# A routed decoder layer: pad rows written behind each expert's last row instead of ahead of time

## The reference

```
x = layernorm(x + attention(x))                      # low rank scores, one score matrix for all 16 heads
e = minimum(ids // 3125, 3)                          # four experts, chosen by the id
x = layernorm(x + silu(x @ ctx[e].T) * (x @ ctx[e].T) @ ctx[e])
probs = softmax(x @ Wr + br);  e2 = argmax(probs)    # four experts, chosen by a router
x = layernorm(x + max(probs) * ((silu(x @ Wg[e2]) * (x @ Wu[e2])) @ Wd[e2]))   # 256 -> 1024 -> 256
```

## Time and profile before

| | us |
|---|---|
| median of 3 runs | 195.73 |
| the 3 runs | 194.76, 195.73, 196.36 |
| the profiled execution | 194.84 |
| its span, first to last instruction | 192.5 |

### The profile page before, as it was taken

The page is one execution under the profiler, slowest core; times in us unless marked ns, Lnnn a source line. Parts: engine busy times, 40 slices in busy tenths (PEclk is TensorE's granted clock), DMA queues, the critical chain, the costliest instruction groups (busy, mean ns, idle before and its releaser), DMA issues.

```text
span 192.5 us, 3892 instructions
## 1 busy us (share of the span) xinstructions
PE 175.1 (91%) x966; PEld 139.4 (72%) x966; DVE 129.8 (67%) x406; ACT 103.4 (54%) x274; POOL 103.0 (53%) x130
## 2 busy tenths in 40 slices
PE   1999999999999799989999999999999999999810
PEld 0877766367888546668888788888888888888610
DVE  3277878768687878536664454444799977888950
ACT  3138687535477654647664855534555423455530
POOL 7000267744917666528772368850688800376783
PEclk9999999999999999999999999999999999999975
DMA  5999999348997222247554005544050000011010
GB/s 163 354 334 418 376 364 346 102 140 232 353 371 295 93 87 64 74 116 215 171 167 163 0 1 177 171 156 158 0 167 0 0 0 3 0 54 60 22 63 24
DMA packets 15605, 29.14 MB, mean 151 GB/s; under 512 B 1758, under 2 KB 12000, under 8 KB 15458
## 3 DMA queue, kind: packets, MB, share of 16 engines
q1 hardware_dynamic: 13856, 25.68, 40.1%
q0 software_dynamic: 1440, 3.22, 4.7%
q10 hardware_dynamic: 290, 0.01, 0.1%
HBM read 20.41 MB, written 9.28 MB: 154 GB/s over the span
## 4 chain that ended last, share of the span: by engine, by line
PE 71%; POOL 11%; issue 7%; DVE 4%; DMA 3%; ACT 1%; POOLq 1%; DVEq 0%; ACTq 0%
PE bank L502 14%; PE bank L504 13%; PE bank L503 13%; POOL out_tokens L491 5%; PE bank L764 4%; PE bank L589 4%; PE bank L685 3%; PE bank L662 3%; POOL rstd L418 3%; PE bank L620 3%; PE bank L516 2%; PE bank L598 2%; PE bank L734 2%; PE bank L510 2%; DMA x_sorted<-buf,slot 1%
## 5 line engine op out<-in xcount | busy, mean ns | idle before, releaser
L414 POOL TENSOR_TENSOR w_lo<-stage,w_hi 128x512 fp32r<-128x512 f32 x40 | 51.3, 1303 | 34.7 <-ACT w_hi L841 29.9
L962 ACT ACTIVATE gate<-bank 128x256 f32<-128x256 f32 x44 | 16.9, 384 | 48.1 <-PE bank L504 48.0
L1264 DVE TENSOR_TENSOR hid<-bank,gate 128x256 f32<-128x256 f32 x44 | 18.7, 425 | 30.2 <-ACT gate L962 29.9
L502 PE MATMUL bank<-w_hi,xr 128*128 x88 | 35.9, 408 | 1.4 <-DVE xr L1217 1.2
L504 PE MATMUL bank<-w_hi,xr 128*128 x88 | 34.8, 395 | 0.0
L503 PE MATMUL bank<-w_lo,xr 128*128 x88 | 34.7, 395 | 0.0
L502 PE MATMUL bank<-w_hi,hT 128*128 x88 | 28.6, 324 | 0.7 <-DVE hT L1269 0.7
L418 POOL TENSOR_TENSOR rstd<-mv,mhalf 128x1 f32<-128x1 f32 x19 | 11.3, 597 | 31.2 <-DVE mv L1103 30.9
L841 ACT ACTIVATE w_hi<-stage 128x512 fp32r<-128x512 f32 x45 | 27.0, 630 | 0.3 <-PE bank L504 0.3
L504 PE MATMUL bank<-w_hi,hT 128*128 x88 | 24.9, 283 | 0.0
L503 PE MATMUL bank<-w_lo,hT 128*128 x88 | 24.8, 282 | 0.0
(11 more groups left out here) (188 smaller groups left out, 328.3 us busy)
## 6 DMA issues: line engine op xcount, KB each, us to landing
stage<-in_w_ffn SPq DMA_DIRECT2D x15, 768.0 KB
rows<-x_sorted SPq DMA_DIRECT2D x22, 132.0 KB, 2.2
x_sorted<-padrow SPq DMA_DIRECT2D x1, 2244.0 KB
x_sorted<-padrow SPq DMA_DIRECT2D x1, 2112.0 KB
buf<-in_x_tok SPq DMA_DIRECT2D x1, 1024.0 KB, 11.3
w_hi<-in_ctx SPq DMA_DIRECT2D x1, 1024.0 KB, 11.9
w_hi<-in_ctxT SPq DMA_DIRECT2D x1, 1024.0 KB
x_sorted<-padrow SPq DMA_DIRECT2D x1, 792.0 KB, 13.1
```

The lines of the kernel that those rows point to most:

```text
L414: g.tensor_tensor(out=lo, in0=src, in1=hi.bitcast(F32), op=ALU.subtract).then_inc(split_lo, 1)
L502: mm(dst, xhi, whi, start=start, stop=False)
L962: a(gate[:, (T + j) % 2, :], fA[j % 2][:, 0:FQ], ACT.Silu).then_inc(silu_done, 1)
L1264: v.tensor_tensor(out=hid[:, (T + j) % 2, :], in0=fA[j % 2][:, FQ:2 * FQ], in1=gate[:, (T + j) % 2, :], op=ALU.mult).then_inc(h_done, 1)
```

## The change

The regions of `scr2` become 1152 rows long (one block more than an expert can fill), and the two large pad transfers go, with POOL's wait for them. One transfer of 128 rows pads the extra block at the end. When all tiles are ranked, DVE copies the four experts' ends (`pR`, row T) into `pad_from` as integers; SP waits for that, loads the four numbers into registers, and issues four transfers of 128 pad rows, one behind each expert's last row. Before it loads tiles 3 to 10 it waits until these have landed. These steps stand in SP's queue between the loads of tiles 0 to 2 and the wait for `row_table` 2.

Since a region now has nine blocks and an expert at most eight, the first row of a block is no longer 128 times its number: `row_tables` multiplies its comparison by `block_rows` (128, and 256 for the last block of an expert) before it sums, one more DVE instruction in each of its two calls. The constants grow by two.

```diff
-REGION = TOKENS
+REGION = TOKENS + P
...
-        CONSTS = 23
+        CONSTS = 25
...
-            pads2 = scr2.rearrange("(p r) c -> p r c", p=P)
-            HALF2 = BLOCKS2 // 2
-            sp.dma_start(pads2[:, 0:HALF2, :], padrow[:].unsqueeze(1).broadcast_to([P, HALF2, ROW])).then_inc(d_init2, 16)
+            sp.dma_start(scr2[(BLOCKS2 - 1) * P:BLOCKS2 * P, :], padrow[:]).then_inc(d_pads, 16)
...
-            sp.dma_start(pads2[:, HALF2:BLOCKS2, :],
-                         padrow[:].unsqueeze(1).broadcast_to([P, BLOCKS2 - HALF2, ROW])).then_inc(d_init2, 16)
...
             for t in range(EARLY):
                 routed_row(t, r[t])
+            sp.wait_ge(pad_table, 1)
+            r = [sp.value_load(pad_from[0:1, e:e + 1], min_val=e * REGION, max_val=e * REGION + TOKENS) for e in range(E)]
+            sp.wait_ge(d_pads, 16)
+            for e in range(E):
+                sp.dma_start(scr2[bass.ds(r[e], P), :], padrow[:]).then_inc(d_pads, 16)
             sp.wait_ge(row_table, 2)
             r = {t: first_row(t) for t in range(EARLY, EARLY + 2)}
+            sp.wait_ge(d_pads, 16 * (1 + E))
             sp.wait_ge(d_scat2[1], 16 * (T - ROUTED))
...
+            const(g.memset(block_rows[:], float(P)))
             pool.wait_ge(consts, const.n)
             g.memset(padrow[:, TOK:TOK + 1], FAR).then_inc(pad_ready, 1)
+            const(g.memset(block_rows[:, :, CHUNKS - 1:CHUNKS], float(P + REGION - TOKENS)))
...
-            pool.wait_ge(d_init2, 32)
...
-                step(v.tensor_reduce(out=block_no[:, a:b], in_=is_slot[:, a:b, :], axis=AX.X, op=ALU.add))
-                v.scalar_tensor_tensor(out=row2[:, a:b], in0=block_no[:, a:b], scalar=float(P), in1=ones_f[:, 0:w],
-                                       op0=ALU.mult, op1=ALU.mult).then_inc(row_table, 1)
-                step(v.tensor_tensor(out=past[:, a:b, :], in0=block_no[:, a:b].unsqueeze(2).broadcast_to([P, w, E - 1]),
+                step(v.tensor_tensor(out=is_slot[:, a:b, :], in0=is_slot[:, a:b, :],
+                                     in1=block_rows[:].rearrange("p e c -> p (e c)").unsqueeze(1).broadcast_to([P, w, BLOCKS]),
+                                     op=ALU.mult))
+                step(v.tensor_reduce(out=first[:, a:b], in_=is_slot[:, a:b, :], axis=AX.X, op=ALU.add))
+                v.tensor_copy(row2[:, a:b], first[:, a:b]).then_inc(row_table, 1)
+                step(v.tensor_tensor(out=past[:, a:b, :], in0=first[:, a:b].unsqueeze(2).broadcast_to([P, w, E - 1]),
...
+            def pad_rows():
+                dve.wait_ge(r_done, len(GROUPS))
+                v.tensor_copy(pad_from[:], pR[:, T, 0:E]).then_inc(pad_table, 1)
...
             choose(4)
             fxlo(0)
+            pad_rows()
             place(4)
             fxlo(1)
             late_tables()
```

More of the change, by code:

```diff
@@ L104, in route_kernel @@
         tile_no1 = sb("tile_no1", [P, T])
+        block_rows = sb("block_rows", [P, E, CHUNKS])
+        pad_from = sb("pad_from", [P, E], I32)
         ones32 = sb("ones32", [P, 3 * BLOCKS])
@@ L129, in route_kernel @@
         step_of = sb("step_of", [P, BLOCKS])
-        block_no = sb("block_no", [P, T])
+        first = sb("first", [P, T])
         past = sb("past", [P, T, E - 1])
@@ L199, in route_kernel @@
             sem(n) for n in ("d_aqk", "d_avo", "d_xT0", "d_xT", "d_x", "d_ids", "d_wr"))
-        d_init1, d_init2 = sem("d_init1"), sem("d_init2")
+        d_init1, d_pads = sem("d_init1"), sem("d_pads")
         d_chunk, d_beside = [sem(f"d_chunk{i}") for i in range(SLOTS)], sem("d_beside")
@@ L229, in route_kernel @@
         mask_ready, r_done, slot_ready = (sem(n) for n in ("mask_ready", "r_done", "slot_ready"))
-        tables, row_table = sem("tables"), sem("row_table")
+        tables, row_table, pad_table = sem("tables"), sem("row_table"), sem("pad_table")
         lexp_done, topw_ready = sem("lexp_done"), sem("topw_ready")
@@ L392, in _ @@
                          channel_multiplier=0, allow_small_or_imprecise_dtypes=True))
-            const(g.iota(expert_from[:], pattern=[[CHUNKS, E - 1]], base=CHUNKS, channel_multiplier=0,
+            const(g.iota(expert_from[:], pattern=[[REGION, E - 1]], base=REGION, channel_multiplier=0,
                          allow_small_or_imprecise_dtypes=True))
```

## The result

The changed kernel takes 197.68 us (median of 15 runs, 196.57 to 198.41) against 195.91 us for the kernel before (15 runs, 194.76 to 199.12): ratio 1.0092, 95% interval 1.0072 to 1.0111, so **+1.8 us** where +0.6 us was forecast. The profiled execution took 197.78 us, its span is 196.0 us. A ratio compares undisturbed executions: those over 1.5% above the fastest of the same kernel are left out, which are 5 of 12 for `loads_only`, 4 of 12 for `transfers_only` and few elsewhere. Further down the same comparison comes out at 1.0094 on one other chip and at 0.9982 and 1.0000 on two more, and that turned out to be the larger part of the matter.

A forecast was written before the change was run, and what follows sets the result against it. The prediction took PE to bound the kernel (71% of the chain that ended last). Traffic 0, constants +0.1 and hand-over +0.5 made +0.6 us, so 195.73 became 196.3 us, range 195.0 to 197.7.

The forecast's parts named there:

- What bounds the kernel, and where the change acts: PE is busy beside the large pad transfers and in phase 3; delay to item 3 at 78 to 84 us moves the end.
- Constants, +0.1: At the kernel's start, two more constants delay PE's first product at 4.19 us: +0.1 us, between 0.05 and 0.3.
- DVE: Added table instructions: 0.30 us early, 0.11 of it passed on; 0.46 late; `fup(2)` at the second hand-over 0.29 us later.
- The traffic, costed at 0: Removing 4.4 MB of large pad writes at 20 to 34 and 46 to 58 us gains 0, at most 1.5 us.
- SP's step, +0.5: Second hand-over: register loads, four pad transfers and their wait put tile 3's load 1.07 us later, its transposes 0.50 us later.
- the pads hold PE up for longer: Rival at the second hand-over: pads land later on shared DMA engines, PE waits 1.7 us; +2.3, 198.0 us; chance 0.17.
- The Trainium skill: Its page on DMA cost, for the pad writes to DRAM: 2.3 us each, making the hand-over 0.7 instead of 0.5 us.
- The clock, 0.04: Rival: PE idles some 1.5 us around item 3, its clock falls to half, 2 us more lost; 198.3 us; chance 0.04.

The follow-up runs named there:

- loads_only: `tables_only` plus SP's wait for the copied ends and its four register loads, without any small pad transfer; ratio 1.0016 to the kernel before (chip 9).
- transfers_only: `tables_only` plus four pad transfers to fixed places in a spare scratch and the wait for them, without register loads; ratio 0.9990 to the kernel before (chip 9).
- dve33: The kernel before plus only DVE's added steps and the two constants, regions and large pad transfers unchanged; ratio 1.0015 to the kernel before (chip 2).
- dve33_again: `dve33` timed again on chip 12; ratio 1.0005 to the kernel before.
- split8: The kernel before with 8 rows in the first large pad transfer and 25 in the second, instead of 16 and 17; ratio 1.0181 (chip 4).
- before_warm: The kernel before with seven products without use on PE; ratio 1.0031 to the kernel before (chip 2).
- before_again: The kernel before, unchanged, timed again for another trace; ratio 0.9987 (chip 4).
- warm: The changed kernel with seven products without use on PE, two ahead of `fth(0)`, five ahead of `fup(2)`; ratio 0.9984 to the kernel before (chip 4).
- after_again: The changed kernel, timed again on chip 2; ratio 0.9982 to the kernel before.
- bulk_back8: `bulk_back` with 8 rows in the first large transfer and 29 in the second; 199.99 us, ratio 1.0271 to the kernel before (chip 4).
- after_third: The changed kernel, timed a third time, on chip 11; ratio 1.0094 to the kernel before.
- tables_only: The changed kernel without SP's step, both large pad transfers and POOL's wait back at 18 and 19 rows; ratio 1.0021 to the kernel before (chip 9).
- bulk_back: The whole changed kernel plus both large pad transfers to a spare scratch and POOL's wait; ratio 1.0198 to the kernel before (chip 9).
- warm_again: `warm` timed again on chip 11; ratio 1.0062 to the kernel before.

## Why the prediction was wrong

**What bounds the kernel, and where the change acts: right.** PE's times in 20 to 34 and 46 to 58 us are the same to 0.01 us, and the distance from tile 3's transpose to the end of the span is 110.5 us before and 110.4 after.

**Constants, +0.1: right** (PE's first product at 4.26 instead of 4.19). **DVE: right, a little low.** The new instruction takes 0.29 us from start to start in the early call (forecast 0.30) and 0.46 in the late one (0.46). In the traces of the kernels with DVE's part alone, D grows from 9.30 to 9.69 or 9.77, so by 0.4 to 0.5 where the forecast had 0.29 for `fup(2)`. With the constants, the median span of `dve33` is 0.7 us longer than before's on chip 2 and that of `dve33_again` 0.55 on chip 12; the forecast's terms for them make 0.4.

**Outside the span: a term that the sum didn't have.** What lies around the span is 2.3 us for the kernel before, on all chips, and 1.7 to 1.8 us for every kernel with the changed tables, `dve33` among them; `split8` and `before_warm` keep 2.3. So some 0.55 us (0.57 between the two profiled executions of the first timing) come back that no view shows, and this is why `dve33`, with a longer span, is only 0.1% above the kernel before. What of the edit does it, I can't tell.

**The traffic, costed at 0: about right for the trace, low for the kernel.** The removed transfers save 0.15 us in B by the trace on which I argued, and nothing in A; by `before_again` they save 0.22 and 0.4. The median span says as much: on chip 2 the changed kernel's is 0.4 us shorter than that of `dve33`, though D is 0.34 longer. On chip 12 it is 0.1 us longer.

**SP's step, +0.5: the step that failed.** On chips 2, 4 and 12 its number was near: I put tile 3's load 7.81 us behind PE's first transpose (80.55 - 72.74), and it stands at 7.80 and 7.83, and at 7.89 in `warm`. That is luck, for it was another wait that came last. The pads landed 1.8 us after their issue, not 2.1, by the least, median and most of `after_again`'s four:

```profile
DMA to landing us min/median/max: 1.7/1.8/1.9
```

The last of them, issued at 77.75, was there at 79.6; what held the load of 80.15 was SP's own row of register loads, which ended at 79.9 us. The two for tiles 3 and 4 took 1.76 us (78.13 to 79.89) where I had 1.14. PE was at tile 3 0.73 to 0.81 us later than before, not 0.50. Only in `bulk_back8` does the trace show the step as forecast: the last pad transfer, issued at 83.19, lands at 85.31, and tile 3's load follows at 85.47.

On the chips with the hold-up the durations that I had taken from the earlier trace rows, 0.57 us for a register load and 0.52 for an issue, did not hold. The last pad transfer was issued 6.96 us behind PE's first transpose instead of 5.56, and tile 3's load at 9.17 (9.20 and 9.40 on chip 11) instead of 7.81. D became 11.4 to 11.8 us, so 2.1 to 2.5 more than before where the forecast had 0.5. In the first trace PE's own way there, through `fup(2)`, was late too: by 1.3 us more than before against its first transpose, where I had 0.29. A third part I had at nothing: E, ahead of phase 3, is 0.6 us longer than in the kernel before on such a chip (14.96 and 15.14 against 14.38), as PE idles behind the early hold-up. With 0.1 for the constants, 0.2 off for the traffic and 0.57 off outside the span that makes 2.0 to 2.6 us by single traces, against 1.8 measured. Of the rivals "the pads hold PE up for longer" (198.0 us, chance 0.17) had nearly the time, and tile 3 did come late: from chips 2, 4 and 12 to chip 11 C and D grow by 1.3 to 1.6 us each, a us for a us. But its reason did not hold. I had looked for it in the DMA engines; no landing is recorded on these chips, but tile 3's load, which waits for all four pads, stands at most 2.2 us behind the last issue, so they can't have landed late. They were issued late, by SP's instructions.

The Trainium skill ("DMA: Bandwidth & Descriptors", the section on the anatomy of one DMA) would have had the pad transfers land later than a read, as writes to DRAM. The runs show no such lead: 1.75 to 2.16 us for the 28 writes that are recorded, with a median of 1.83, and a median of 2.1 for the reads of the same size. (The section describes transfers that GpSimd issues; these are SP's.) The measurement decides.

**The clock, 0.04: too low.** It fell in about a third of the executions on these chips, and in the profiled one it made the six products of `fup(2)` 0.43 us apart, where those of `fup(0)` are 0.23 apart: 6 x 0.20 = 1.2 us, of which some 0.5 are left behind the late tile. Of the median it holds 0.1 to 0.4 us. I had argued from one execution that 1.13 us of idle time in 78 to 84 us did no harm; idle times of 0.50 and 1.07 us within 2.5 us did. But idle time alone doesn't decide: 0.54 and 0.93 us at 64 and 66 us left the clock up in the changed kernel's first trace, and 0.61 and 0.93 at the same place brought it down in `after_third`.

**What stays open.** Why some chips have the hold-up. That SP's step costs much on such a chip and little elsewhere is shown by `tables_only` and `bulk_back` on chip 9 (2.1 us of D) and by `dve33` and `after_again` on chip 2 (0.34 us); but no run there took the register loads alone out of the changed kernel. That the hold-up comes with POOL's scatters is read from the times in the traces (the first timing's, `after_third`, `warm_again`, `bulk_back`, `loads_only`), not shown by taking them away. What ACT's and DVE's late releases cost apart from SP's late loads wasn't separated either.

## What to carry to other kernels

A queue's own instructions are part of a path: a step with a register load ahead of each transfer has little to do with how long the transfers take, and four in a row with what follows can use up a slack that each part alone leaves (from PE's first transpose to tile 3's load, 6.9 us for either part, 7.8 for both without the hold-up and 9.2 to 9.7 with it). Where the row number can be had otherwise, or the loads made ahead, do so. Traffic that nobody waits for is free only up to an edge: with 12% more of it PE waited 1.6 us in the trace of `tables_only`; ask how far away the edge is before calling it free. And a difference of 1% should be timed on more than one chip: here it was +0.9% in two timings and 0 or less in two others.

## What the runs showed of the hardware

- In three of the six timings, SP's register instructions came in groups about 0.7 us apart for 3.4 us while two indirect DMAs of POOL ran; in the three others the same instructions beside the same DMAs took their usual 0.15 and 0.27 us. ACT took up a finished product 1.2 us late in that time (0.47 in the trace of the kernel before, 0.04 in `before_again` and `after_again`).
- In all eight traces of those three timings DVE took up a finished result of PE 1.0 to 1.7 us late while an earlier indirect DMA ran, in the unchanged kernel too; in all twelve others it took 0.11 us.
- A DVE edit with two more constants took 0.5 to 0.6 us away from the time outside the span, on all chips.
- A write of 128 x 1056 bytes to DRAM issued by SP landed in 1.75 to 2.16 us (28 transfers in seven traces).
- Where TensorE's granted clock fell from 1.00 to 0.50 between the first and the last 10 us of a span, it stayed there for 3.4 us: eleven times in eight of the twenty traces. In three of these places PE had idled just ahead for 0.50 + 1.07 us (the changed kernel, at 81 us), 1.51 + 0.28 (`after_third`, at 87) and 1.63 (`tables_only`, at 42).
